# The sine product of the leaf rotations moves from VectorE to GpSimd, into a tile of its own

## The reference

```python
deg = jnp.sum(A, axis=-1)
d_isqrt = jax.lax.rsqrt(deg)
Lap = deg[..., :, None] * jnp.eye(n) - A
Lap_norm = d_isqrt[..., :, None] * Lap * d_isqrt[..., None, :]
_, U = jnp.linalg.eigh(Lap_norm)
agg = jnp.einsum('bmn,bmd->bnd', U, features)
h = jax.nn.relu(jnp.einsum('bnd,hd->bnh', agg, W0) + b0)
out = jnp.einsum('bnh,oh->bno', h, W1) + b1
ret = jnp.einsum('bnm,bmo->bno', U, out)
```

## Time and profile before

| | us |
|---|---|
| median of 3 runs | 5151.7 (5149.34 to 5155.43) |
| the profiled execution | 5160.19 |
| its span in the trace | 5157.9 |
| DVE busy in it | 4163.5 |
| PE busy | 2378.0 |
| ACT busy | 1313.2 |
| POOL busy | 122.0 |

### The profile page before, as it was taken

One profiled execution on the slowest core, in us unless ns is written; L12 is line 12 of the kernel. 1 busy time (PEld: TensorE's weight loads), 2 busy tenths in 40 slices (PEclk: granted clock), 3 DMA queues, 4 the chain that ended last, 5 costly groups with the idle time before them and its releaser, 6 DMA issues.

```text
span 5157.9 us, 57427 instructions
## 1 busy us (share of the span) xinstructions
PE 2378.0 (46%) x15702; PEld 1593.0 (31%) x15702; DVE 4163.5 (81%) x18604; ACT 1313.2 (25%) x4350; POOL 122.0 (2%) x53
## 2 busy tenths in 40 slices
PE   0555555555526717519349063344105821020399
PEld 0222222233324314215124063243105820020266
DVE  4788878888779999999999888686996979989522
ACT  0000000011113233242342233122442412224154
POOL 0000000000000000000000010010003100000000
PEclk9766666665556857758668576676557965555699
DMA  6000000000110000000000112005000030020120
GB/s 144 14 15 25 25 16 19 19 22 25 30 31 9 9 9 17 0 9 17 9 1 0 17 31 45 0 9 124 0 0 9 17 124 0 0 114 0 49 66 17
DMA packets 142060, 140.50 MB, mean 27 GB/s; under 512 B 28445, under 2 KB 128426, under 8 KB 134826
## 3 DMA queue, kind: packets, MB, share of 16 engines
q1 hardware_dynamic: 141738, 136.97, 9.8%
HBM read 110.43 MB, written 26.41 MB: 27 GB/s over the span
## 4 chain that ended last, share of the span: by engine, by line
DVE 60%; PE 27%; DMA 5%; issue 4%; ACT 3%; SPq 1%; DVEq 0%; ACTq 0%; PEldq 0%
PE psum L2038 7%; PE psum L1678 5%; DVE big_a L381 2%; DVE gvec L385 2%; DVE big_b L1107 2%; PE psum L2062 2%; DMA big_b<-rows_dram 1%; DVE vt L529 1%; PE psum L2240 1%; DVE big_b L716 1%; DMA vt<-pairs_dram 1%; DVE sc_t L951 1%; DVE big_b L707 1%; DVE big_b L711 1%; DVE big_a L953 1%
## 5 line engine op out<-in xcount | busy, mean ns | idle before, releaser
L2038 PE MATMUL psum<-big_a 128*32 128x508 f32 (+59 forms) x4032 | 443.7, 606 | 54.1 <-issue 50.9
L1627 PE MATMUL psum<-plane,big_a 128*128 128x128 f32 x192 | 50.2, 430 | 608.8 <-ACT big_a L1543 587.2
L2013 PE MATMUL psum<-plane,big_b 128*128 128x128 f32 x126 | 54.6, 433 | 442.7 <-DVE big_b L396 442.1
L2038 PEld LDWEIGHTS psum<-big_a 128*32 128x32 f32 x4032 | 174.3, 157 | 255.0 <-issue 175.5
L1678 PE MATMUL psum<-big_b 128*128 128x512 f32 x544 | 245.5, 613 | 0.0
L2234 PE MATMUL psum<-plane,big_b 128*128 128x128 f32 x192 | 37.7, 378 | 443.2 <-DVEq L1308 426.7
L2224 PE MATMUL psum<-big_b 128*128 128x128 f32 x384 | 71.7, 372 | 349.7 <-ACT big_b L2138 349.7
L1627 PEld LDWEIGHTS psum<-plane,big_a 128*128 128x128 f32 x192 | 36.0, 220 | 622.6 <-ACT big_a L1543 599.6
L1837 DVE TENSOR_REDUCE f_ln<-psum 128x4 f32<-128x512 f32 x32 | 22.1, 689 | 233.6 <-PE psum L1952 157.8
L1996 ACT COPY big_a<-psum 128x64 f32<-128x64 f32 x109 | 29.1, 267 | 662.7 <-PE psum L2047 662.7
L2219 PE MATMUL psum<-vt,big_b 128*128 128x128 f32 (+1 forms) x384 | 72.3, 375 | 261.1 <-ACT big_b L1330 261.1
(11 more groups left out here) (729 smaller groups left out, 9270.4 us busy)
## 6 DMA issues: line engine op xcount, KB each, us to landing
big_a<-rows_dram SPq DMA_DIRECT2D x4, 4096.0 KB, 13.9
vt<-pairs_dram SPq DMA_DIRECT2D x504, 32.0 KB
big_a<-rows_dram SPq DMA_DIRECT2D x4, 2048.0 KB, 17.3
pairs_dram<-big_a SPq DMA_DIRECT2D x252, 32.0 KB, 1.8
big_a<-rows_dram SPq DMA_DIRECT2D x2, 3072.0 KB, 15.6
big_b<-rows_dram SPq DMA_DIRECT2D x2, 3072.0 KB, 22.5
big_b<-adj SPq DMA_DIRECT2D x2, 2048.0 KB, 17.6
big_b<-adjT SPq DMA_DIRECT2D x2, 2048.0 KB, 39.5
```

The source lines that it names most:

```text
L1627: ins = t.transpose(psum[0:parts, bank, g * N:(g + 1) * N], src(g), ident)
L2013: t.transpose(psum[:, 1, 0:SLOTS], x_rows[0:SLOTS, k % 2, :], whole).then_inc(S("x_node_ps"), 1)
L2038: ins = t.matmul(psum[i * SPAN:i * SPAN + MW, 0, 0:4 * wide], v_masked[:, i, q * MW:(q + 1) * MW], anode[:, g:g + 4, k + 1:N + 2 * u], sta ...
```

## The change

POOL gets the product of `src` with the sines. It waits for the announcement of the cosines and sines and writes into a tile of its own, `v_w` (graphs 0 to 7 of `vt`). DVE's line 530 goes, and `rotate` waits for the semaphore `sines_applied` before the product that overwrites `src`. `v_w` must be zero for the first rotation, so DVE waits for its clearing (`cleared` at 4) once; at the end of the stage POOL clears it again. Besides, the loads of the Laplacian count on the semaphore `adj_g_in` instead of one of their own.

```diff
+        v_w = vt[:, 0:8, :].rearrange("p a b -> p (a b)")
...
             v.sem_inc(S("rotated"), 1)
+            v.wait_ge(S("cleared"), 4)
+            v.sem_inc(S("sines_applied"), 1)
 
             def rotate(src, dst, expanded):
 
                 lp(v.tensor_tensor(rows_of(v_u), rows_of(src), each_row(1), ALU.mult))
                 v.wait_ge(S("rotated"), expanded)
                 lp(v.tensor_tensor_scan(dst, v_s, v_u, 0.0, ALU.mult, ALU.add))
-                lp.go(v.tensor_tensor(rows_of(v_u), rows_of(src), each_row(2), ALU.mult))
-                lp.after(lp.n)
+                v.wait_ge(S("sines_applied"), expanded)
                 lp(v.tensor_tensor(rows_of(src)[:, :, :, dn], rows_of(dst)[:, :, :, dn], each_row(1)[:, :, :, up], ALU.mult))
-                lp(v.tensor_tensor(rows_of(dst)[:, :, :, dn], rows_of(src)[:, :, :, dn], rows_of(v_u)[:, :, :, up], ALU.add))
+                lp(v.tensor_tensor(rows_of(dst)[:, :, :, dn], rows_of(src)[:, :, :, dn], rows_of(v_w)[:, :, :, up], ALU.add))
...
-            t.wait_ge(S("anode_in"), 64)
+            t.wait_ge(adj_g_in, 128)
...
             p.memset(vt[:, 0:32, :], 0.0).then_inc(S("cleared"), 1)
+            by_row = lambda ap: ap.rearrange("p (q r k) -> p q r k", q=LQ, r=LEAF)
+
+            def sines(nth, src):
+                p.wait_ge(S("rotations_ready"), nth)
+                p.tensor_tensor(by_row(v_w), by_row(src), over(l_cs[:, 2], LEAF, 2), ALU.mult).then_inc(S("sines_applied"), 1)
+
+            with p.Fori(0, GROUPS) as i:
+                for u in range(STAGES):
+                    sines(i * STAGES + (u + 1), (v_b, v_a)[u % 2])
+            sines(SWEEPS + 1, v_b)
             p.wait_ge(leaves_ready, 1)
+            p.memset(vt[:, 0:8, :], 0.0)
             p.memset(vt[:, 32:, :], 0.0).then_inc(S("cleared"), 1)
```

More of the change, by code:

```diff
@@ L2302, in _ @@
                 for rows in strips[c]:
-                    sy.dma_start(anode[rows, :, 0:N], lap_dram[:, rows, :].rearrange("g i j -> i g j")).then_inc(S("anode_in"), 16)
+                    sy.dma_start(anode[rows, :, 0:N], lap_dram[:, rows, :].rearrange("g i j -> i g j")).then_inc(adj_g_in, 16)
             sy.wait_ge(S("tri_started"), 2)
```

## The result

The changed kernel takes 5174.24 us in the median of 5 runs (5173.01 to 5177.52), against 5151.18 us for the kernel before in its 5: ratio 1.0045, 95% interval 1.003 to 1.006. It is 23 us slower; the forecast was 5175. A second set on another occasion gave 1.0058 (1.0037 to 1.0078).

A forecast was written before the change was run, and what follows sets the result against it. VectorE's instruction list was taken to bound the leaf stage. Terms -52.9 + 88.2 - 12.5 + 0.5 = +23.3 us on the 5151.7 us median gave 5175 us, range 5160 to 5198.

The forecast's parts named there:

- The bound: Leaf stage: DVE is busy 1339.3 of 1438.5 us, so its own instruction list sets the stage's length.
- The removal: Rotation in the leaf stage: dropping DVE's line 530 saves 1.26 us, 42 times, 52.9 us in all.
- The duration: GpSimd's new 128x1024 product in the leaf stage: 2.35 us each, 2.8 as the upper end.
- The stop: DVE behind each announcement: stands still during GpSimd's product, losing 2.15 us, 41 times, 88.2 us.
- What softens it: DVE's waits in longer sweeps: second convolution gives back 10.7 us, ScalarE's gates 1.8, together -12.5 us.
- TensorE is not touched: Convolution waits: TensorE's chain stays as it was, so DVE coming 2.7 us later shrinks each of four waits equally.
- The ends: End of the leaf stage: the added clearing of vt's eight graphs delays the leaf vectors' load, +0.5 us.
- Rival 1: Leaf stage: GpSimd runs beside DVE and only the removed line 530 counts, 5117 us; chance 0.07.
- Rival 2: Leaf stage: DVE loses only about 1.3 us per GpSimd product, 5152 us; chance 0.09.
- Rival 3: GpSimd's product takes 2.8 us and DVE loses all of it, 5196 us; chance 0.16 for 5188 and above.
- rival 4: Rotation: GpSimd's product comes late and DVE waits at line 532, if over 16 us; chance under 0.02.

The follow-up runs named there:

- experiment 1: Changed kernel with VectorE's own sine product put back and used, GpSimd's product made besides and read by nothing: 5213.48 us, ratio 1.0124 to the kernel before.
- experiment 2: Changed kernel without any sine product, GpSimd only raising the semaphore, leaf vectors written as identities: 5109.94 us, ratio 0.9928 to the kernel before.
- experiment 3: Changed kernel without a sine product, GpSimd instead clearing the 128x1024 tile at each announcement: 5113.8 us, ratio 0.9925 to the kernel before.
- experiment 5: Changed kernel without a sine product, GpSimd instead copying the 128x1024 leaf vectors at each announcement: 5134.05 us, ratio 0.9968 to the kernel before.
- experiment 6: Changed kernel with GpSimd's product asked for at the head of the next sweep, not behind the announcement: 5154.37 us, ratio 1.0014 to the kernel before.
- experiment 7: Changed kernel with ScalarE making the product as 64 instructions, GpSimd idle: 5207.89 us, ratio 1.0114 to the kernel before.
- experiment 4: Changed kernel with the sine product split, GpSimd making two of four leaves and VectorE the other two: 5159.03 us, ratio 1.0018 to the kernel before.
- experiment 8: VectorE makes the product except in sweeps 6, 7 and 8, where GpSimd does, asked for at the sweep's head: 5129.21 us, ratio 0.9954 to the kernel before.
- experiment 10: VectorE makes the product except in sweeps 2, 6, 7 and 8, where GpSimd does: 5134.6 us, ratio 0.9968 to the kernel before.
- experiment 11: Second run of the kernel with GpSimd's product only in sweeps 6, 7 and 8: 5136.95 us, ratio 0.9978 to the kernel before.
- Experiment 9: VectorE makes the product except in sweeps 0, 4 and 9, where GpSimd does: 5161.05 us, ratio 1.0023 to the kernel before.

## Why the prediction was right, point by point

- **The bound.** The stage is DVE's: what DVE is spared, loses and waits gives the stage's length (84.5 less 22.0 gives 62.5 for 60.4; 52.9 less 7.9 and 2.0 gives 43.0 for 44.8). Shown by experiments 1 and 2.
- **The removal, 52.9 us.** 1.26 a rotation, as read.
- **The duration, 2.35 us.** Measured 2.349. The choice by the row with the longest runs was right; the mean of 4.52 over the older products would have been twice too long, and the Trainium skill's figure (GPSIMD Engine Reference, § Performance versus the Vector engine), which is for an addition of 2048 elements and halved makes an estimate of 2.25, somewhat short.
- **The stop, 88.2 us.** Measured 2.06 a time for 2.15: 84.4. It comes from GpSimd's reading (experiments 3 and 5) and lasts as long as its instruction less 0.2 to 0.3 us (2.06 of 2.35, 0.98 of 1.26, 0.84 of 1.04). About 0.15 of the 0.29 is that the product had begun 0.15 us before the blocked instruction; line 530 in experiment 6, which starts 0.02 us into the product, loses 2.19.
- **A wrong detail.** I put the announcement right behind line 583 and expected the stop at the line 719 that follows 0.10 us later. Line 585 is reached only in the step after it, behind line 716, so the stop falls on the next 719, 0.9 us later. Nothing was priced by it.
- **What softens it, 12.5 us.** The sum, 11.6 in the first profile (17.9 + 5.5 to 11.8), is right by luck, for neither part is. The wait for the convolution gave 6.1 and not 10.7, because TensorE's chain took 4.5 us longer than before, and the waits fell to 11.8 where about 7 was forecast. (Two of the four waits were 2.5 us long and could not give 2.7 each, either.) The wait for the gates gave 5.5 and not 1.8. It depends on TensorE's clock behind the convolution and not only on the length of one sweep; in experiment 2 it is gone although the sweeps got shorter. "TensorE is not touched" is true of its program, but its pace differs from group to group. In the second profile both waits together gave 6.5.
- **The ends.** From SP's first store of the leaves to the load it is 4.12 us before (2941.91 to 2946.03) and 4.51 after: +0.4 for +0.5.
- **Rival 1 (beside one another)** would have had the removal's worth, 5110 as experiment 2 shows; its mechanism exists, but only where DVE has at most one input in SBUF or where GpSimd only writes. **Rival 2 (half a stall)** falls for this change; experiment 6 is the version that gives it, by another cause than the one I named. **Rival 3** falls by the product's 2.35, **rival 4** because no wait stands at line 534.
- The sum of the profile: -52.9 + 84.4 - 11.6 = +19.9, and 2.0 us of small new gaps (last section) give 21.9 for a stage that became 21.0 us longer, with 0.4 behind it; the medians differ by 23.1. That this is 0.2 us from the forecast of 23.3 is luck too: the stop was put 3.8 us too high and what softens it 0.9, the small gaps were not foreseen, and two sets of runs differ by more than that (23 and 28 us). What was right by reading is the removal, the duration and the stop.

## What to carry to other kernels

Work that goes from VectorE to GpSimd is not free because GpSimd is idle: read first how long VectorE's instructions last while a GpSimd instruction of that kind runs, and look for a tiny one that takes as long as GpSimd's. If GpSimd reads SBUF, the move paid in these runs only where VectorE, for as long as the product lasts, waits for another engine, or has one of its two inputs in PSUM (a single-input instruction ran on too); the same twelve products were worth -9 to -21 us there and +10 elsewhere. To price it, take GpSimd's duration less 0.2 to 0.3 us as VectorE's loss, as measured here for 512 and 1024 elements, against what VectorE is spared. And where the bounding engine waits for TensorE, look at the granted clock of TensorE's stretch before pricing the wait: the same work took 42.5 to 48.5 us here.

## What the runs showed of the hardware that was not expected

- A VectorE product of one PSUM and one SBUF input runs at its own pace beside a GpSimd product (0.64 us each for 128x512, as without), while one of two SBUF inputs, even 128x4, stands for the whole rest of it.
- A VectorE instruction of a single SBUF input keeps its pace too (the reciprocal of 128x16, 0.25 us beside the product and without it).
- TensorE's granted clock in the same stretch of work differs between groups and executions (0.61, 0.65 or 0.70 in the mean), and with it VectorE's wait for the convolution, by up to 9 us over the four groups, against the kernel before.
- All versions in which DVE makes the sine product in no sweep (the changed kernel and experiments 2, 3, 5, 6 and 7) show four gaps of 0.5 us ahead of a sweep's first instruction, one in each group behind sweep 0, in all 2.0 us, which the kernel before and the experiments 1, 4, 8, 10 and 11 don't list. Experiment 9 has them too, where DVE makes the product in seven sweeps of ten but not in sweep 0. They go with DVE's instruction list in sweep 0 and not with GpSimd's work, since experiment 2 has them with GpSimd idle. The cause stays open.
